# One-hot operands of an adjacency build: source split into tile and place, eight edge tiles at a time

## The chip, the cores and the metric

The kernel runs on one core of a Trainium2 chip. TensorE (PE in the profile, PEld for its weight loads), VectorE (DVE), ScalarE (ACT), GpSimd (POOL) and SyncE (SP) have instruction streams of their own and wait for each other by semaphores. The metric is the device time of one execution in microseconds, and the time of a kernel is the median over its runs.

## The reference

Two layers of a graph network with 1250 nodes, 768 features and 40,000 edges; each layer has a graph part, an attention part and a feed-forward part. The edges come sorted by destination. What the change touches is how the edges are used. In the first layer's graph part an edge counts as often as it occurs (and each node has a loop), in the second it counts with its weight:

```python
src, dst, edge_weight            # (40000,) each; dst is sorted
# layer 0, GAT: softmax over the edges that end in a node
e = leaky_relu(al_s[src] + al_d[dst], 0.2)
ex = exp(e - segment_max(e, dst)[dst])
out = segment_sum(h[src] * (ex / segment_sum(ex, dst)[dst])[:, :, None], dst)
# layer 1, GCN: weighted sums
deg = segment_sum(edge_weight, col) + 1.0
norm = rsqrt(deg)[row] * edge_weight * rsqrt(deg)[col]
agg = segment_sum(norm[:, None] * x[row], col)
```

The kernel turns the edges into two dense 1250 x 1250 matrices first, the number of edges from each source to each destination (CT) and the sum of their weights (WA, with ones on the diagonal), and works with those from there on.

## The kernel before

The edges lie as 313 tiles of 128 (`ET`), one edge per partition: `src_c`, `dst_c` and the weight as three bf16 parts `w_c[0..2]` that sum up to it, a column per edge tile. `NB` = 40 blocks of `SPREAD` = 8 tiles follow each other. As the edges are sorted, the destinations of a block lie in a window of `WIN` = 38 nodes, which begins at `base`; a test before the loop (`viol`, `flag`) sees whether that holds, and otherwise all engines take another loop, in which each block goes through all edges. Both loops call the same functions.

For one block, each engine in a loop over 20 pairs of blocks (`par` 0 and 1 are the two halves of the buffers):

- DVE, `destinations`: one operation (L1645) compares the destinations of the eight tiles with the window, which gives a one-hot of 8 x 38 columns, and three (L1651) multiply it with the three weight parts. So a tile has 4 x 38 = 152 columns (`KINDS` = 4). `next_block` (L1664) moves the window. `sources`, for seven of the eight tiles (L1660): the source of each edge against the numbers 0 to 1249, a one-hot of 1250 fp16 columns, into a ring of eight places.
- ACT, `source`: the one-hot of the eighth tile by two operations over 1250 columns (L1304, L1306).
- PE, `edge_tiles` (L890): for each tile and each of the ten groups of 125 source nodes, the one-hot of the group is the stationary operand and the 152 destination columns stream past it. That is 10 matmuls a tile and 80 a block, summed up in four banks of PSUM per half.
- ACT, `stage_block`: copies the block's sums from PSUM to `stage` (L1316, L1318), when PE is through and POOL has left the half.
- POOL, `unstage`: adds the three weight parts up (L749, L752) and adds count and weight into CT and WA at the window (L750, L756), four operations over 125 x 380.

What sets the order: PE waits tile by tile for its one-hot (`src_hot`, and `src_hot_act` for the eighth); DVE waits for `tiles_done`, so that a place in the ring is free; ACT waits for PE and POOL, POOL for ACT. Before the loop stands the setup: edges are loaded, turned by PE and copied (L1598 to L1637), with DVE waiting for its own last step by `chain`, while POOL fills constants and zeroes CT and WA (L731, L732). Behind the loop follows a layer norm: DVE's statistics of x (L1689) need nothing of the loop; its writing (L1701) goes to the memory in which the one-hots lie and waits for the last block's copy.

Of the kernel before, what the change touches and what calls it, by code (L numbers as in the profile page):

```python
# [46 lines left out]
RING = 8  # L47
# [168 lines left out]
def build(nc: bass.Bass, A, out):  # L216
    packets, pieces, last, packet_at = make_plan()

    with ExitStack() as ctx:
# [61 lines left out]
        def ecut(n):  # L281
# [21 lines left out]
        rawf = ecut(9 * P).rearrange("p (a r e) -> p a r e", a=3, r=3)  # L303
        ecut(2 * NT * KINDS * WIN - 18 * P)
        stage = xt_r[0:TILE, stage0:stage0 + 2 * NT * KINDS * WIN].rearrange("p (b j k w) -> p b j k w", b=2, j=NT, k=KINDS)
        oh_src = h_r[:, 0:RING * 625].bitcast(FP16).rearrange("p (s n) -> p s n", s=RING)
        oh_dst = h_r[:, 5000:5000 + SPREAD * KINDS * WIN].bitcast(BF16)\
            .rearrange("p (b t k w) -> p b t k w", b=2, t=SPREAD, k=KINDS)
# [391 lines left out]
        def _(pool):  # L700
# [27 lines left out]
            pool.sem_inc(ev("staged"), 4)  # L728
# [14 lines left out]
            def unstage(b, par, done):  # L743

                at = pool.value_load(basei[0:1, bass.ds(b, 1)], min_val=0, max_val=LAST)
                c = bass.ds(at, WIN)
                pool.wait_ge(ev("staged"), done * 2 + 6)
                k = stage[:, par]
                pool.tensor_tensor(k[:, :, 3, :], k[:, :, 3, :], k[:, :, 2, :], ALU.add).then_inc(ev("unst_b"), 1)  # L749
                pool.tensor_tensor(CT[:, :, c], CT[:, :, c], k[:, :, 0, :], ALU.add).then_inc(ev("unst_a"), 1)  # L750
                pool.wait_ge(ev("unst_b"), done + 1)
                pool.tensor_tensor(k[:, :, 3, :], k[:, :, 3, :], k[:, :, 1, :], ALU.add).then_inc(ev("unst_c"), 1)  # L752
                pool.wait_ge(ev("unst_a"), done + 1)
                pool.wait_ge(ev("unst_c"), done + 1)
                pool.wait_ge(ev("unstaged"), done + 2)
                pool.tensor_tensor(WA[:, :, c], WA[:, :, c], k[:, :, 3, :], ALU.add).then_inc(ev("unstaged"), 1)  # L756
# [87 lines left out]
        def _(pe):  # L844
# [32 lines left out]
            def bank(par, q):  # L877
                return ps[0:TILE, 2 * par + q // 2, 512 * (q % 2):512 * (q % 2) + 512]

            def edge_tiles(par, n, fresh):  # L880

                for u in range(SPREAD):
                    if u < SPREAD - 1:
                        pe.wait_ge(ev("src_hot"), n * (SPREAD - 1) + (u + 1))
                    else:
                        pe.wait_ge(ev("src_hot_act"), n + 1)
                    s = u % RING
                    for j in range(NT):
                        o = KINDS * WIN * (j % 3)
                        mm = pe.matmul(bank(par, j // 3)[:, o:o + KINDS * WIN], oh_src[:, s, j * TILE:j * TILE + TILE],  # L890
                                       oh_dst[:, par, u, :, :], start=(fresh and u == 0 and j % 3 == 0), stop=False,
                                       skip_group_check=True)
                    mm.then_inc(ev("tiles_done"), 1)

            def open_block(par, b):

                pe.wait_ge(ev("staged"), b * 2 + 2)

            def clear(par):
                for q in range(4):  # L900
                    w = KINDS * WIN * (3 if q < 3 else 1)
                    pe.matmul(bank(par, q)[:, 0:w], zero16[:, 0:TILE], zero16[:, 0:w], start=True, stop=False,
                              skip_group_check=True)

            with pe.If(flag == 0):
                with pe.Fori(0, NB // 2) as bp:
                    for par in range(2):
                        b = bp * 2 + par
                        open_block(par, b)
                        pe.wait_ge(ev("dst_hot"), b + 1)  # L910
                        edge_tiles(par, b, True)
            with pe.Else():
# [377 lines left out]
        def _(act):  # L1290
# [10 lines left out]
            def source(col, n):  # L1301

                act.wait_ge(ev("tiles_done"), n * SPREAD + CREDIT)
                act.activation(far, iota_src, ACT.Abs, bias=src_n[:, bass.ds(col, 1)]).then_inc(ev("src_far"), 1)  # L1304
                act.wait_ge(ev("src_far"), n + 1)
                act.activation(oh_src[:, RING - 1, :], far, ACT.Relu, bias=onesc, scale=-1.0)\  # L1306
                   .then_inc(ev("src_hot_act"), 1)

            def stage_block(par, b, tiles):
# [944 lines left out]
```

## Time and profile before

| | us |
|---|---|
| median of 3 runs | 3161.21 (3160.83 to 3163.68) |
| the profiled execution | 3162.54 |
| its span, first to last instruction | 3160.8 |
| setup, to DVE's first L1645 | 35.2 |
| adjacency loop, to the end of DVE's last L1660 | 306.7 |
| rest | 2818.9 |

All figures are of one core. In a row of windows the stretch comes first, then its length, then the busy time and the number of operations of PE, PEld, DVE, ACT and POOL, then the granted clock of TensorE as a share of full speed (1.00 is 2.4 GHz, 0.50 is 1.2 GHz), the busy share of the DMA engines and GB/s. In a timeline a row has start, length, engine, line, operation, output and inputs, shape and count; operations of one line that follow each other are one row, and the records of two neighbours overlap a little, so that the pace of an engine is read from start to start.

### The profile page before, as it was taken

What the parts mean: (1) busy time and instruction counts of PE and PEld (TensorE: products, weight loads), DVE (VectorE), ACT (ScalarE), POOL (GpSimd) and SP (SyncE); (2) the same over time, 40 slices, a digit from 0 to 9 for tenths busy, and PEclk for the clock granted to TensorE, in tenths of its full rate; (3) what the DMA queues carried; (4) which work ended last, traced back from release to release, by engine and by line L of the source; (5) the groups of instructions that cost most, each with busy time, mean ns of one, the idle gap of its engine ahead of it and who ended that gap; (6) DMA issues with size and microseconds to landing.
All of it is one profiled execution on the core that took longest, in us unless ns stands there. A gap on an engine that the chain in (4) does not pass through costs nothing.

```text
span 3160.8 us, 33593 instructions
## 1 busy us (share of the span) xinstructions
PE 2801.1 (89%) x13527; PEld 1971.8 (62%) x13527; DVE 1612.7 (51%) x2217; ACT 923.6 (29%) x974; POOL 333.0 (11%) x314
## 2 busy tenths in 40 slices
PE   4777899999989889699956989996879999899999
PEld 4777565688876556477743855553457777555555
DVE  8999679889973444311133230004267777522220
ACT  3666310077751232111110011011054444321110
POOL 5556230000000011100030000000000000000000
PEclk9999999999999899799976999997989999999999
DMA  9700431121030301477755100000020100200000
GB/s 248 265 0 0 110 94 59 42 71 57 34 64 6 84 7 52 140 250 261 259 150 115 33 17 0 30 30 29 0 80 27 40 27 29 105 10 10 10 10 10
DMA packets 123619, 226.60 MB, mean 72 GB/s; under 512 B 18535, under 2 KB 91788, under 8 KB 123006
## 3 DMA queue, kind: packets, MB, share of 16 engines
q1 hardware_dynamic: 107746, 178.79, 19.0%
q0 software_dynamic: 15760, 46.20, 4.6%
q8 instruction: 84, 1.38, 0.2%
q14 instruction: 29, 0.24, 0.0%
HBM read 158.92 MB, written 66.01 MB: 71 GB/s over the span
## 4 chain that ended last, share of the span: by engine, by line
PE 72%; DVE 18%; issue 3%; DMA 3%; ACT 2%; DVEq 1%; POOL 1%; SPq 0%; ACTq 0%; POOLq 0%
PE ps L939 20%; PE ps L1283 13%; PE ps L1267 13%; DVE arena L1660 5%; PE ps L1163 4%; PE ps L1129 4%; PE ps L956 4%; PE ps L1175 4%; DVE arena L1790 2%; DVE arena L1791 2%; PE ps L1216 1%; DVE small L1689 1%; PE ps L1208 1%; PE ps L1039 1%; DMA arena<-in_x_dram 1%
## 5 line engine op out<-in xcount | busy, mean ns | idle before, releaser
L939 PE MATMUL ps<-arena 128*125 128x384 f32 x2160 | 719.8, 496 | 28.3 <-DVE arena L2124 12.8
L939 PEld LDWEIGHTS ps<-arena 128*125 128x125 f32 x2160 | 412.4, 192 | 324.7 <-issue 34.5
L1283 PE MATMUL ps<-arena 128*125 128x384 f32 x1280 | 414.5, 488 | 14.2 <-DVE arena L2164 14.2
L1267 PE MATMUL ps<-arena 128*128 128x312 f32 (+1 forms) x1536 | 407.2, 428 | 15.2 <-DVE arena L2164 15.2
L1267 PEld LDWEIGHTS ps<-arena 128*128 128x128 f32 x1536 | 292.5, 191 | 129.6 <-issue 16.8
L1283 PEld LDWEIGHTS ps<-arena 128*125 128x125 f32 x1280 | 241.0, 188 | 187.6 <-issue 16.1
L1295 ACT ACTIVATE arena<-ps 128x750 f32<-128x750 f32 (+4 forms) x175 | 133.2, 792 | 722.0 <-PE ps L939 206.3
L890 PE MATMUL ps<-arena 128*125 128x152 bf16 x3200 | 244.2, 234 | 67.2 <-DVE arena L1660 65.6
L2164 DVE SCALAR_TENSOR_TENSOR arena<-arena 128x1250 f32<-128x1250 f32 (+1 forms) x170 | 231.4, 1383 | 114.5 <-PE ps L1267 110.9
L890 PEld LDWEIGHTS ps<-arena 128*125 128x125 f16 x3200 | 222.8, 138 | 88.6 <-DVE arena L1660 87.7
L1727 DVE SCALAR_TENSOR_TENSOR arena<-ps,arena 125x768 f32<-125x768 f32 x30 | 28.7, 956 | 379.1 <-PE ps L1283 291.9
L1660 DVE TENSOR_SCALAR arena<-arena 128x1250 f16<-128x1250 f16 x280 | 218.2, 850 | 0.0
L1039 PE MATMUL ps<-arena 125*125 125x97 f32 x1600 | 182.9, 276 | 5.7 <-DVE arena L1791 5.7
L1039 PEld LDWEIGHTS ps<-arena 125*125 125x125 f32 x1600 | 181.0, 192 | 9.0 <-DVE arena L1791 6.9
L2080 DVE TENSOR_TENSOR arena<-ps,arena 128x768 f32<-128x768 f32 x34 | 32.6, 958 | 271.3 <-PE ps L1175 271.3
L956 PE MATMUL ps<-arena 128*128 128x312 f32 (+7 forms) x544 | 156.6, 449 | 3.2 <-ACT arena L1295 2.2
L1129 PE MATMUL ps<-arena 125*125 125x385 f32 (+1 forms) x400 | 136.4, 497 | 11.3 <-POOL arena L821 11.3
L1783 DVE CUSTOM_DVE_ANT_0 arena<-arena 125x1250 bf16<-125x1250 bf16 x90 | 131.4, 1460 | 23.6 <-DMA arena<-al_src 21.0
L1163 PE MATMUL ps<-arena 128*128 128x256 f32 x612 | 136.8, 383 | 1.1 <-ACT arena L1295 1.1
L1175 PE MATMUL ps<-arena 128*128 128x384 f32 x408 | 134.5, 486 | 0.8 <-ACT arena L1295 0.8
L956 PEld LDWEIGHTS ps<-arena 128*128 128x128 f32 (+3 forms) x544 | 102.7, 191 | 52.1 <-issue 18.2
L1163 PEld LDWEIGHTS ps<-arena 128*128 128x128 f32 x612 | 117.7, 193 | 21.1 <-issue 1.5
(296 smaller groups left out, 2875.2 us busy)
## 6 DMA issues: line engine op xcount, KB each, us to landing
arena<-in_L_ffn_W_dram SPq DMA_DIRECT2D x34, 1152.0 KB, 7.0
xs_rows<-arena SPq DMA_DIRECT2D x1, 30720.0 KB, 99.5
arena<-xs_rows SPq DMA_DIRECT2D x17, 768.0 KB, 7.9
y_rows<-arena POOLq DMA_DIRECT2D x34, 384.0 KB, 3.3
arena<-in_kw_dram SPq DMA_DIRECT2D x24, 512.0 KB, 5.7
arena<-al_dst POOLq DMA_DIRECT2D x18, 625.0 KB, 4.9
arena<-in_kw_dram SPq DMA_DIRECT2D x6, 1536.0 KB, 9.9
arena<-in_x_dram SPq DMA_DIRECT2D x2, 3600.0 KB
```

Source lines behind the costliest of these rows:

```text
L890: mm = pe.matmul(bank(par, j // 3)[:, o:o + KINDS * WIN], oh_src[:, s, j * TILE:j * TILE + TILE], oh_dst[:, par, u, :, :], start=(fresh an ...
L939: mm = pe.matmul(slot(g)[0:TILE, 512 * half:512 * half + HALF], xt[:, k, i * TILE:i * TILE + TILE], w[:, k, :], start=(k == 0), stop=(k == ...
L956: mm = pe.matmul(slot(g)[0:rows, 512 * b:512 * b + w], stat, mov[:, lo + b * w:lo + b * w + w], start=(t == 0), stop=(t == len(terms) - 1))
L1039: mm = pe.matmul(slot(g)[0:TILE, 512 * (j // 5) + 97 * (j % 5):512 * (j // 5) + 97 * (j % 5) + 97], AT[m % AHEAD][:, j * TILE:j * TILE + T ...
L1129: mm = pe.matmul(slot(g)[0:TILE, 512 * b:512 * b + w], AT2[i][:, j * TILE:j * TILE + TILE], H769[:, i, lo:lo + w], start=(i == 0), stop=(i ...
L1163: mm = pe.matmul(slot(g)[:, 0:TAU], w1s[t % 2][:, k, f * P:f * P + P], xsT[t % 2][:, k, :], start=(k == 0), stop=(k == KT - 1))
L1175: mm = pe.matmul(slot(g)[:, 512 * b:512 * b + HALF], hTt[t % 2][:, f, h * P:h * P + P], w2s[t % 2][:, f, b * HALF:b * HALF + HALF], start= ...
L1267: mm = pe.matmul(slot(g)[:, 512 * b:512 * b + wd_], w[:, r % 2, ORDER[p], o * P:o * P + P], feat[place(f)][:, lo + b * wd_:lo + b * wd_ + ...
L1283: mm = pe.matmul(slot(g)[0:TILE, 512 * b:512 * b + HALF], fv[:, q, :], w2c[m][q][:, b * HALF:b * HALF + HALF], start=(p == 0 and q == 0), ...
L1295: give(act.activation(dst, src, func, **kw), g)
L1660: dve.tensor_scalar(oh_src[:, u % RING, :], iota_src, src_c[:, bass.ds(col + u, 1)], None, ALU.is_equal).then_inc(ev("src_hot"), 1)
L2164: return dve.scalar_tensor_tensor(out=out_, in0=in_, scalar=edge, in1=of, op0=op, op1=ALU.mult)
```

## The change

The one-hot of a source is split. A source s is in tile g = s // 125 and at place s - 125 g. The stationary operand is now the one-hot of the place alone (125 columns), once plain and three times multiplied with a part of the weight; the streamed operand is the one-hot of 38 g + (destination - window), 10 x 38 = 380 columns (`SPOTS`). A tile so has 4 matmuls of 380 columns instead of 10 of 152. The three weight parts are summed up in PSUM (the second bank of the half), so that a half holds two banks, one for the count and one for the weight, and POOL has two additions instead of four. The parts of the weight are kept as f32 (`w_p`), rounded through bf16.

DVE makes the four kinds of stationary operand for eight tiles at a time, by one comparison and three multiplications over 8 x 125 = 1000 elements, and then the eight streamed operands one by one. ACT makes no one-hots any more. The setup gets `group` (nine steps, each adding one where the source is at or over 125 t), `member` and `spot_of`. Both halves have a place of their own for all eight tiles, so that DVE waits for the tiles two blocks back.

```diff
@@ pool: constants, and into the matrices @@
-            own.step(pool.iota(iota_src, [[1, NODES]], base=0, channel_multiplier=0,
+            own.step(pool.iota(spots, [[1, SPOTS]], base=0, channel_multiplier=0,
                                allow_small_or_imprecise_dtypes=True))
-            own.step(pool.iota(iota_0, [[1, WIN]], base=0, channel_multiplier=0,
+            own.step(pool.iota(within, [[1, TILE]], base=0, channel_multiplier=0,
                                allow_small_or_imprecise_dtypes=True))
...
-                pool.wait_ge(ev("staged"), done * 2 + 6)
+                pool.wait_ge(ev("staged"), done + 3)
                 k = stage[:, par]
-                pool.tensor_tensor(k[:, :, 3, :], k[:, :, 3, :], k[:, :, 2, :], ALU.add).then_inc(ev("unst_b"), 1)
-                pool.tensor_tensor(CT[:, :, c], CT[:, :, c], k[:, :, 0, :], ALU.add).then_inc(ev("unst_a"), 1)
-                pool.wait_ge(ev("unst_b"), done + 1)
-                pool.tensor_tensor(k[:, :, 3, :], k[:, :, 3, :], k[:, :, 1, :], ALU.add).then_inc(ev("unst_c"), 1)
+                pool.tensor_tensor(CT[:, :, c], CT[:, :, c], k[:, 0], ALU.add).then_inc(ev("unst_a"), 1)
                 pool.wait_ge(ev("unst_a"), done + 1)
-                pool.wait_ge(ev("unst_c"), done + 1)
                 pool.wait_ge(ev("unstaged"), done + 2)
-                pool.tensor_tensor(WA[:, :, c], WA[:, :, c], k[:, :, 3, :], ALU.add).then_inc(ev("unstaged"), 1)
+                pool.tensor_tensor(WA[:, :, c], WA[:, :, c], k[:, 1], ALU.add).then_inc(ev("unstaged"), 1)
@@ tensor @@
                 for u in range(SPREAD):
...
-                    for j in range(NT):
-                        o = KINDS * WIN * (j % 3)
-                        mm = pe.matmul(bank(par, j // 3)[:, o:o + KINDS * WIN], oh_src[:, s, j * TILE:j * TILE + TILE],
-                                       oh_dst[:, par, u, :, :], start=(fresh and u == 0 and j % 3 == 0), stop=False,
-                                       skip_group_check=True)
+                    pe.wait_ge(ev("hot"), n * SPREAD + (u + 1))
+                    for k in range(KINDS):
+                        mm = pe.matmul(bank(par, min(k, 1)), oh_src[:, par, u, k, :], oh_spot[:, par, u, :],
+                                       start=(fresh and u == 0 and k < 2), stop=False, skip_group_check=True)
                     mm.then_inc(ev("tiles_done"), 1)
@@ scalar: source() is gone, one copy of 2 x 380 from PSUM @@
-                act.activation(dst[:, 0:9 * w].rearrange("p (b n) -> p b n", b=3), src[:, 0:3, 0:3 * w], ACT.Copy)\
+                act.activation(stage[:, par].rearrange("p k j w -> p k (j w)"), banks_of(par), ACT.Copy)\
                    .then_inc(ev("staged"), 1)
-                act.activation(dst[:, 9 * w:10 * w], src[:, 3, 0:w], ACT.Copy).then_inc(ev("staged"), 1)
@@ vector: setup @@
-            own.step(dve.tensor_scalar(src_n, ps[:, 0, 0:NB * SPREAD], -1.0, None, ALU.mult))
+            own.step(dve.memset(group, 0.0))
             own.settle()
 
-            chain(dve.tensor_copy(w_c[0], w_f))
-            chain(dve.tensor_tensor(w_f, w_f, w_c[0], ALU.subtract))
-            chain(dve.tensor_copy(w_c[1], w_f))
-            chain(dve.tensor_tensor(w_f, w_f, w_c[1], ALU.subtract))
-            chain(dve.tensor_copy(w_c[2], w_f))
+            for k in range(3):
+                chain(dve.tensor_copy(w_16, w_f))
+                chain(dve.tensor_copy(w_p[k], w_16))
+                if k < 2:
+                    chain(dve.tensor_tensor(w_f, w_f, w_p[k], ALU.subtract))
+            for t in range(1, NT):
+                chain(dve.scalar_tensor_tensor(out=group, in0=src_c, scalar=float(t * TILE), in1=group,
+                                               op0=ALU.is_ge, op1=ALU.add))
+            chain(dve.scalar_tensor_tensor(out=member, in0=group, scalar=-float(TILE), in1=src_c,
+                                           op0=ALU.mult, op1=ALU.add))
...
-            dve.tensor_scalar(iota_b, iota_0, base[:, 0:1], None, ALU.add).then_inc(ev("next_block"), 1)
+            chain(dve.scalar_tensor_tensor(out=grouped(spot_of), in0=grouped(group), scalar=float(WIN), in1=grouped(offset),
+                                           op0=ALU.mult, op1=ALU.add))
@@ vector: the block; destinations(), sources() and next_block() are gone @@
+            def one_hots(par, col, tile0, ring, spot, n):
+
+                dve.wait_ge(ev("tiles_done"), tile0 + (SPREAD - ring + CREDIT))
+                wide = [P, SPREAD, TILE]
+                dve.tensor_tensor(oh_src[:, par, :, 0, :], within.unsqueeze(1).broadcast_to(wide),
+                                  member[:, bass.ds(col, SPREAD)].unsqueeze(2).broadcast_to(wide), ALU.is_equal)\
+                   .then_inc(ev("plain"), 1)
+                dve.wait_ge(ev("plain"), n + 1)
                 for k in range(3):
+                    dve.tensor_tensor(oh_src[:, par, :, 1 + k, :], oh_src[:, par, :, 0, :],
+                                      w_p[k][:, bass.ds(col, SPREAD)].unsqueeze(2).broadcast_to(wide), ALU.mult)
+                for u in range(SPREAD):
+                    dve.tensor_scalar(oh_spot[:, par, u, :], spots, spot(u), None, ALU.is_equal).then_inc(ev("hot"), 1)
```

`keys`, which makes the same numbers for the other loop (unsorted edges), isn't shown.

How the instructions stand, first on DVE in the first block of the loop. ISA and REGISTER_ALU are steps of the engine's own sequencer; `ev_tiles_done` counts tiles that PE is through with. Before, to the second L1660:

```order
L1645 ISA [waits ev_tiles_done]
L1645 TENSOR_TENSOR arena<-arena 128x8x38
L1651 ISA [waits ev_dst_plain]
L1651 TENSOR_TENSOR arena<-arena 128x8x38
L1651 ISA
L1651 TENSOR_TENSOR arena<-arena 128x8x38
L1651 ISA
L1651 TENSOR_TENSOR arena<-arena 128x8x38
L1664 ISA
L1664 TENSOR_SCALAR arena<-arena 128x38
L1659 REGISTER_ALU
L1660 ISA [waits ev_tiles_done]
```

Behind it stand seven of the 128x1250 operations, each with such a wait. After, to the second of eight L1637:

```order
L1629 ISA [waits ev_tiles_done]
L1629 TENSOR_TENSOR arena<-arena 128x8x125
L1632 REGISTER_ALU
L1634 ISA [waits ev_plain]
L1634 TENSOR_TENSOR arena<-arena 128x8x125
L1634 ISA
L1634 TENSOR_TENSOR arena<-arena 128x8x125
L1634 ISA
L1634 TENSOR_TENSOR arena<-arena 128x8x125
L1637 ISA
L1637 TENSOR_SCALAR arena<-arena 128x380
L1637 ISA
```

The operations with two tensor inputs grow from 304 to 1000 elements; the one-source operations behind them are eight over 380 instead of seven over 1250, and only the block's first step waits for PE.

On POOL, one block of the loop. Before:

```order
L749 TENSOR_TENSOR arena<-arena 125x10x38 [waits ev_staged]
L750 ISA
L750 TENSOR_TENSOR arena<-arena 125x10x38
L751 REGISTER_ALU
L752 TENSOR_TENSOR arena<-arena 125x10x38 [waits ev_unst_b]
L755 REGISTER_ALU [waits ev_unst_c,ev_unst_a]
L756 ISA [waits ev_unstaged]
L756 TENSOR_TENSOR arena<-arena 125x10x38
```

After:

```order
L753 ISA [waits ev_staged]
L753 TENSOR_TENSOR arena<-arena 125x10x38
L754 REGISTER_ALU
L755 REGISTER_ALU [waits ev_unst_a]
L756 ISA [waits ev_unstaged]
L756 TENSOR_TENSOR arena<-arena 125x10x38
```

The two additions within `stage` are gone, the two into the matrices remain.

## Rows read from the trace of the kernel before

**Rows 1.** The page, busy tenths of DVE in 40 slices of 79 us.

```profile
DVE  8999679889973444311133230004267777522220
```

**Rows 2.** Windows: the adjacency loop; columns as told above.

```profile
35.19:341.90 306.71, 242.41 (x3176) 221.13 (x3177) 300.85 (x481) 188.47 (x178) 180.27 (x156) 0.99 0.35 118
```

**Rows 3.** Waits from 37 to 342 us: total, times, longest.

```profile
ACT arena L1316 <- PE ps L890: 114.5, 39, 6.6
...
PE ps L890 <- DVE arena L1660: 65.6, 97, 5.5
```

**Rows 4.** Timeline of DVE, the first two blocks of the loop.

```profile
35.19 0.48 DVE L1645 TENSOR_TENSOR arena<-arena 128x304 bf16<-128x304 f32 x1 [1.45 <-issue]
35.81 1.25 DVE L1651 TENSOR_TENSOR arena<-arena 128x304 bf16<-128x304 bf16 x3
36.97 0.24 DVE L1664 TENSOR_SCALAR arena<-arena 128x38 f32<-128x38 f32 x1
37.12 3.27 DVE L1660 TENSOR_SCALAR arena<-arena 128x1250 f16<-128x1250 f16 x7
40.31 0.47 DVE L1645 TENSOR_TENSOR arena<-arena 128x304 bf16<-128x304 f32 x1
...
45.64 0.48 DVE L1645 TENSOR_TENSOR arena<-arena 128x304 bf16<-128x304 f32 x1
```

**Rows 5.** Single lines: count, ns min/median/max, first and last start.

```profile
L1645 DVE TENSOR_TENSOR arena<-arena x40: 459/461/1267, 35.2 to 334.3; 128x304 bf16<-128x304 f32 x40
...
L1660 DVE TENSOR_SCALAR arena<-arena x280: 529/544/1285, 37.1 to 341.4; 128x1250 f16<-128x1250 f16 x140
```

**Rows 6.** Timeline from 54 to 57 us, DVE and POOL.

```profile
54.47 1.24 POOL L752 TENSOR_TENSOR arena<-arena 125x380 f32<-125x380 f32 x1
54.77 1.27 DVE L1645 TENSOR_TENSOR arena<-arena 128x304 bf16<-128x304 f32 x1
...
56.18 1.06 DVE L1651 TENSOR_TENSOR arena<-arena 128x304 bf16<-128x304 bf16 x1
```

**Rows 7.** Timeline of PE, the first blocks of the loop.

```profile
37.72 16.94 PE L890 MATMUL ps<-arena 128*125 128x152 bf16 x220 [5.47 <-DVE arena L1660]
```

**Rows 8.** Timeline of DVE in the setup.

```profile
27.01 0.56 DVE L1609 TENSOR_TENSOR arena<-arena 128x384 f32<-128x384 f32 x1
27.61 0.36 DVE L1610 CAST arena<-arena 128x384 bf16<-128x384 f32 x1
...
29.76 0.33 DVE L1623 TENSOR_SCALAR arena<-arena 128x320 f32<-128x320 f32 x1
...
32.48 0.20 DVE L1630 TENSOR_TENSOR arena<-arena 128x40 f32<-128x40 f32 x1
32.71 0.26 DVE L1631 SCALAR_TENSOR_TENSOR arena<-arena,small 128x40 f32<-128x40 f32 x1
33.02 0.18 DVE L1634 TENSOR_SCALAR arena<-arena 128x40 f32<-128x40 f32 x1
```

**Rows 9.** Groups by line, 344 to 350 us: busy us, mean ns, idle before.

```profile
L1689 DVE BATCH_NORM_STATS2 small<-arena 125x6 f32<-125x384 f32 x14 | 6.5, 539 | 0.0
...
L756 POOL TENSOR_TENSOR arena<-arena 125x380 f32 x1 | 1.0, 994 | 0.3 <-POOL arena L752 0.3
L750 POOL TENSOR_TENSOR arena<-arena 125x380 f32 x1 | 0.9, 873 | 0.0
```

**Rows 10.** Timeline of POOL in the setup.

```profile
2.96 1.18 POOL L711 IOTA arena<- 128x1250 f16 x1
...
10.74 10.98 POOL L732 MEMSET arena<- 125x12800 f32 x1
```

**Rows 11.** Windows around the fall of TensorE's clock in the loop.

```profile
52.60:59.39 6.79, 4.51 (x62) 4.05 (x61) 6.65 (x11) 5.78 (x6) 4.61 (x5) 1.00 1.05 363
59.39:62.80 3.41, 3.41 (x31) 3.41 (x30) 3.41 (x4) 1.85 (x2) 3.08 (x4) 0.50 1.04 360
62.80:335.00 272.20, 214.53 (x2834) 194.18 (x2833) 267.05 (x424) 167.22 (x158) 163.24 (x141) 1.00 0.29 98
```

More of the change, by code:

```diff
@@ L46 @@
 KINDS = 4
-RING = 8
+SPOTS = NT * WIN
 CREDIT = 32
@@ L284, in ecut @@
             return xt_r[:, eo[0] - n:eo[0]]
-        iota_src = ecut(625).bitcast(FP16)
+        spots = ecut(SPOTS // 2).bitcast(FP16)
+        within = ecut(64).bitcast(FP16)[:, 0:TILE]
         src_c = ecut(ECOLS)
         dst_c = ecut(ECOLS)
-        w_c = [ecut(ECOLS // 2).bitcast(BF16) for _ in range(3)]
+        w_p = [ecut(ECOLS) for _ in range(3)]
         w_f = ecut(ECOLS)
-        src_n = ecut(SPREAD * NB)
-        far = ecut(NODES // 2).bitcast(FP16)
+        w_16 = ecut(ECOLS // 2).bitcast(BF16)
+        group = ecut(ECOLS)
+        member = ecut(ECOLS)
+        offset = ecut(ECOLS)
         viol = ecut(ECOLS)
-        iota_0 = ecut(WIN)
-        iota_b = ecut(WIN)
+        spot_of = ecut(ECOLS)
+        spot8 = ecut(2 * SPREAD).rearrange("p (b t) -> p b t", b=2)
+        out8 = ecut(SPREAD)
+        off8 = ecut(SPREAD)
         zero16 = ecut(256).bitcast(BF16)
@@ L302, in build @@
         raw = ecut(9 * P).rearrange("p (a r e) -> p a r e", a=3, r=3)
[L303 to L308, printed above, removed]
+        stage = xt_r[0:TILE, stage0:stage0 + 4 * SPOTS].rearrange("p (b k j w) -> p b k j w", b=2, k=2, j=NT)
+        ecut(max(0, 4 * SPOTS - 9 * P))
+        rawf = h_r[:, 7040 - 9 * P:7040].rearrange("p (a r e) -> p a r e", a=3, r=3)
+        oh_src = h_r[:, 0:4000].bitcast(BF16).rearrange("p (b t k n) -> p b t k n", b=2, t=SPREAD, k=KINDS)
+        oh_spot = h_r[:, 4000:7040].bitcast(BF16).rearrange("p (b t n) -> p b t n", b=2, t=SPREAD)
         CT = ct_r[0:TILE, 0:6400].bitcast(FP16).rearrange("p (t n) -> p t n", t=NT)
@@ L1299, in _ @@
             flag = act.value_load(flagi[0:1, 0:1], min_val=0, max_val=EDGES)
[L1301 to L1307, printed above, removed]
             def stage_block(par, b, tiles):
@@ L1322, in _ @@
                     for par in range(2):
-                        source((bp * 2 + par) * SPREAD + (SPREAD - 1), bp * 2 + par)
                         stage_block(par, bp * 2 + par, SPREAD)
@@ L1327, in _ @@
                     for par in range(2):
-                        with act.Fori(0, CHUNKS) as ch:
-                            source(ch * SPREAD + (SPREAD - 1), (bp * 2 + par) * CHUNKS + ch)
                         stage_block(par, bp * 2 + par, SPREAD * CHUNKS)
@@ new lines, in keys @@
+            def keys(par, col, b, n):
+                own8 = ev("keys")
+                dve.tensor_scalar(off8, dst_c[:, bass.ds(col, SPREAD)], base[:, bass.ds(b, 1)], None, ALU.subtract)\
+                   .then_inc(own8, 1)
+                dve.wait_ge(own8, n * 5 + 1)
+                dve.tensor_scalar(out8, off8, 0.0, None, ALU.is_lt).then_inc(own8, 1)
+                dve.wait_ge(own8, n * 5 + 2)
+                dve.scalar_tensor_tensor(out=out8, in0=off8, scalar=float(WIN), in1=out8, op0=ALU.is_ge, op1=ALU.add)\
+                   .then_inc(own8, 1)
+                dve.scalar_tensor_tensor(out=off8, in0=group[:, bass.ds(col, SPREAD)], scalar=float(WIN), in1=off8,
+                                         op0=ALU.mult, op1=ALU.add).then_inc(own8, 1)
+                dve.wait_ge(own8, n * 5 + 4)
+                dve.scalar_tensor_tensor(out=spot8[:, par, :], in0=out8, scalar=-4096.0, in1=off8, op0=ALU.mult, op1=ALU.add)\
+                   .then_inc(own8, 1)
+                dve.wait_ge(own8, n * 5 + 5)
@@ L1669, in _ @@
                         b = bp * 2 + par
[L1670 to L1672 removed]
+                        one_hots(par, b * SPREAD, b * SPREAD, 2 * SPREAD, lambda u: spot_of[:, bass.ds(b * SPREAD + u, 1)], b)
             with dve.Else():
@@ L1678, in _ @@
                             n = b * CHUNKS + ch
-                            destinations(par, ch * SPREAD, n, n * SPREAD + CREDIT, b)
-                            sources(ch * SPREAD, n * SPREAD)
-                        next_block(b)
+                            keys(par, ch * SPREAD, b, n)
+                            one_hots(par, ch * SPREAD, n * SPREAD, SPREAD, lambda u: spot8[:, par, u:u + 1], n)
             norms = [0]
```

58 lines of the change are left out of this document (13 added, 45 removed).

## The prediction

> **What bounds the kernel now.** I read the page's slices first: VectorE (DVE) is busy 8 to 9 tenths of the first four slices [rows 1]. The stage in which the change lies, the adjacency loop, runs from 35.19 to 341.89 us, 306.7 us for 40 blocks of eight edge tiles; in it DVE is busy 300.9 us, PE 242.4, POOL 180.3, ACT 188.5 [rows 2]. Second, the waits of that stretch: PE waits 65.6 us for L1660, ACT 114.5 for PE [rows 3], and the view has no row in which DVE waits for anyone. So the loop goes at DVE's pace, and what counts is the sum of DVE's steps in a block, with whatever stretches them.
>
> Third, what stretches them. Before POOL has work, a block takes DVE 5.12 us and one with the loop's branch 5.33 (starts of L1645 at 35.19, 40.31, 45.64) [rows 4], 5.23 in the mean. Later, (334.3 - 45.64)/37 = 7.80 us [rows 5]. The operations are the same. The reader is to see the difference in two places: L1660 takes 529 ns at least and 1285 at most, L1645 459 and 1267 [rows 5]; and at 54.77 us an L1645 lasts until 56.04, 0.33 us beyond the end (55.71) of the POOL operation L752 that was there first, and the L1651 behind it takes 1.06 us, where three of them undisturbed take 1.25 [rows 4]. A DVE operation with POOL at work before it waits until POOL is done, one with two sources as well. The four POOL operations of a block cost (7.80 - 5.23)/4 = 0.64 us of DVE time each.
>
> **PE.** A block has the same columns before (80 x 152) and after (32 x 380), 12,160. Before, 220 matmuls in a row took 16.94 us [rows 7], 6.16 us a block. Longer ones have fewer starts, so 6.16 is the upper bound; at 2.4 GHz and a column a cycle 5.07 would be the lower. Both lie under DVE's old block and its new one: hidden behind DVE. ACT drops its two 1250-element operations and copies 760 elements in place of 1368 and 152: its waits are for PE [rows 3], so it is off the path before, and after all the more.
>
> **DVE in the new block, with POOL away.** Two-source operations: 384 elements take 0.560 us, 40 take 0.200 [rows 8], 1.047 ns an element, and the old 304 with bf16 and with f32 inputs take 0.47 to 0.48 alike [rows 4]; the new ones read a broadcast f32 operand as well. From 304 to 1000 elements is 0.73 us more.
> - The comparison L1629: old step with the wait behind it 0.62 us (35.19 to 35.81), new 1.35.
> - Three multiplications L1634: old step (36.97 - 35.81)/3 = 0.387, new 1.12 each, 3.35.
> - Eight spot one-hots L1637 of 380 fp16 elements, one source. The 1250-element steps are (40.31 - 37.12)/7 = 0.456 us, the 38-element step 0.15 [rows 4]: 0.252 ns an element, so 0.15 + 342 x 0.252 = 0.236 us each, 1.89. That is the lower bound; f32 one-source operations (320 elements 0.33, 40 elements 0.18 [rows 8]) have 0.53 ns an element, 0.33 us each; at the two-source rate it would be 0.51. I take 0.236: input and output are 2 bytes wide as in L1660, only that the output is bf16.
> - The next-block step (L1664, 0.15) goes.
>
> Sum 6.59, with the branch's (5.33 - 5.12)/2 = 0.10 it is 6.69 us, against 5.23. By its own work DVE thus loses 1.46 us a block: seven operations at four elements in a nanosecond give way to 4000 elements at one.
>
> **What POOL gives back.** Two of four POOL operations go (L749, L752); left are the additions into the matrices, L750 (now L753) and L756, 0.87 and 0.99 us undisturbed [rows 9]. They have the shape of the two that go, so I take the old 0.64 us each, 1.29 a block. Bounds: a start-to-start of 56.18 - 54.77 = 1.41 where 0.62 was undisturbed, 0.79 each [rows 4, 6]; below, 0.34, if half of the hold falls into times in which DVE waits anyway (the 0.3 us behind the comparison). Steady block: 6.69 + 1.29 = 7.98 us. Saved are two collisions, 1.29 us; lost 1.46. The first two blocks run without POOL, as before: 2 x 6.69 + 38 x 7.98 = 316.6 us, **+9.9**.
>
> A DVE operation reading one source outside the fast modes isn't stretched: L1689 keeps 539 ns while POOL works [rows 9]. The Trainium skill (SBUF — State Buffer, Who interferes with whom) has the rule: a VectorE operation with two SBUF inputs contends with a GpSimd operation that reads SBUF, whoever starts first keeps the port for its whole length, and an operation with one input outside the two-port modes doesn't. Rows 6 and 9 agree. By the page's "whole length" the two would cost 0.87 and 0.99 us, the block 8.55, the sum 3200; the rows have less, since DVE's own gaps take a part.
>
> **Setup.** DVE's chain from 24.7 to 35.2 us stands ahead of the loop with nearly every step waiting for the one before [rows 8]. Added: ten three-operand operations over 384 elements, at a step of 0.60 (27.01 to 27.61) and perhaps 0.06 more (L1631 0.26 against L1630 0.20): 6.3; one over 320, 0.5; three casts like L1610, 0.36 and the gap of 0.04, 1.2. Removed: L1636, a step like that of L1664, 0.15; L1605 and the memset in its place I take as even. Together +7.9. POOL's iota over 1250 elements (1.18 us) and one over 38 become 380 and 125: 0.94 ns for each of 783 fewer elements, up to 0.7 us, and DVE's second cast waits for the end of POOL's memset at 21.72 (10.74 + 10.98) [rows 10], so -0.7. **+7.2**.
>
> **Behind the loop** nothing is gained: DVE's statistics (L1689, fourteen in 6.5 us [rows 9] and twenty in all, then the mean and root) are some 10 us of work of its own before it writes where the one-hots lie; PE's last block, at most 6.2 us, and the copy of ACT fit under that.
>
> Sum: +9.9 + 7.2 = +17.1 on the profiled execution's 3162.5 (span 3160.8 and 1.7 around it): 3179.6. That execution lies 1.3 us above the median, so **3178 us**. DVE waits for PE only two blocks back (16 tiles), which 6.2 us of PE work in 7.98 never reaches.
>
> **Rivals.**
> 1. *POOL collides less.* It works about 2 us a block, and its operations could fall into the wait behind the comparison or the gaps of the one-hots. The sum is -31.9 us + 76 x the cost of one. At 0.34 each the block is 7.37 and the time 3155, at 0.15 each 7.0 and 3141. The result is within 0.2% between steady blocks of 7.37 and 7.69 (0.34 to 0.50 each), and break-even is 7.53, 0.42 each. For it: in a block of mostly long operations POOL waits at a boundary more often, and one of four boundaries is the wait of 0.3. Against it: the old loop paid 0.64 with gaps of the same number, and L1645 and L1651 were delayed in full [rows 6]. Faster, below 7.37: 0.10; within: 0.14.
> 2. *The spot one-hots miss the fast rate* (bf16 out of fp16). At 0.33 each +0.75 a block, 3208; at 0.51 each +2.2, 3266. No row has this pair of types. 0.07.
> 3. *PE's clock falls and PE becomes the bound.* With PE busy 4.51 of 6.79 us (66%) the clock fell to half (1.2 GHz) from 59.39 to 62.80 us, with 79% it stayed at full for 272 us [rows 11]. The new loop has 64 to 77%. At half clock the columns need 10.13 us a block: 40 x 10.13 = 405, 3267. Against it: that low stretch ended by itself, PE being busy in all of it [rows 11]; PE needs only 5.07/7.98 = 64% of full clock on average. [...] 0.04.
> 4. *The change doesn't do what it says*, the loop taken being the one for unsorted edges, 40 times as many tiles: far over 10,000 us. The test on the edges is unchanged. Under 0.01.
>
> **How the numbers follow.** The forecast, 3168 to 3200 by collision costs of 0.50 to 0.93, has 0.65; the rivals 0.24, 0.07 and 0.04. A measurement here can tell 0.2%, 6.3 us, from no change. Slower by more: 0.65 + 0.11 = 0.76; same 0.14; faster 0.10. Range 3152 to 3204: below it 0.08, above it some 0.11.
>
> **What would show it.** Step by step in the profile after: L1629 about 1.2 us undisturbed and up to 2.0 beside POOL; L1634 1.17; L1637 about 0.3 us long and 0.24 from start to start (0.33 or 0.51 is rival 2); starts of L1629 7.98 apart; DVE's first L1629 at 42.3 us; PE waiting for L1637 about 2 us a block and DVE for nobody. A block under 7.4 us would make me wrong on POOL; PE's clock under 0.65 in the stage with DVE waiting for PE is rival 3.

## The result

| | us |
|---|---|
| before, median of 9 runs | 3161.92 (3156.88 to 3163.68) |
| after, median of 9 runs | 3170.94 (3165.07 to 3174.91) |
| ratio, 95% interval | 1.0028 (1.0018 to 1.0039) |
| the profiled execution of after, its span | 3169.12, 3167.4 |

The changed kernel is slower by 9 us, 0.28%. The forecast was 3178 with a range of 3152 to 3204, slower by more than 0.2%; the direction and the range hold, the size was nearly twice as large (+17 against +9).

The page's slices of DVE, the granted clock below it, in the place of [rows 1]:

```profile
DVE  8999779979983454411124140003267777522220
...
PEclk9998899999999899799976999998989999899999
```

DVE is as full as before in the first four slices, and the clock, at 9 in all of the first five slices before, shows 8 in the fourth and the fifth. The loop and the rest as windows (length, busy us and operations of PE, PEld, DVE, ACT, POOL, then the clock), in the place of [rows 2]:

```profile
41.94:351.46 309.52, 239.02 (x1258) 185.19 (x1259) 303.82 (x481) 56.76 (x59) 110.48 (x77) 0.91 0.32 111
351.46:3167.40 2815.94, 2554.82 (x10338) 1749.33 (x10336) 1294.39 (x1710) 734.40 (x795) 127.39 (x126) 0.94 0.22 66
```

The loop takes 309.5 us instead of 306.7: DVE is busy in nearly all of it, while the busy time of ACT fell from 188.5 to 56.8 and that of POOL from 180.3 to 110.5. The setup ends at 41.94 instead of 35.19. The two are +2.8 and +6.75, +9.6 together, against +9.0 by the medians; the rest differs by 3 us in this pair of executions (2818.9 and 2815.9), which is inside the spread of the runs.

The waits from 40 to 350 us, in the place of [rows 3]:

```profile
ACT arena L1295 <- PE ps L885: 251.5, 39, 11.1
...
PE ps L885 <- DVE arena L1637: 73.7, 38, 8.3
```

The view still has no row in which DVE waits for another engine. The first blocks on DVE, with POOL not yet at work, in the place of [rows 4]:

```profile
41.94 1.21 DVE L1629 TENSOR_TENSOR arena<-arena 128x1000 bf16<-128x1000 f16 x1 [1.35 <-issue]
43.29 3.42 DVE L1634 TENSOR_TENSOR arena<-arena 128x1000 bf16<-128x1000 bf16 x3
46.63 1.92 DVE L1637 TENSOR_SCALAR arena<-arena 128x380 bf16<-128x380 f16 x8
48.46 1.20 DVE L1629 TENSOR_TENSOR arena<-arena 128x1000 bf16<-128x1000 f16 x1
...
54.97 1.19 DVE L1629 TENSOR_TENSOR arena<-arena 128x1000 bf16<-128x1000 f16 x1
```

A block is 6.52 and 6.51 us, and its parts are 1.35, 3.34 (1.113 each) and 1.83 (0.229 each). Later blocks take (344.9 - 54.97)/37 = 7.84 us in the mean; most of them are close to one of 6.5, 7.9 and 9.0 us, by how many POOL operations fall into them. Single lines (ns min/median/max, first and last start), in the place of [rows 5]:

```profile
L1629 DVE TENSOR_TENSOR arena<-arena x40: 1186/1192/1205, 41.9 to 344.9; 128x1000 bf16<-128x1000 f16 x40
L1634 DVE TENSOR_TENSOR arena<-arena x120: 1184/1196/1926, 43.3 to 348.4; 128x1000 bf16<-128x1000 bf16 x120
L1637 DVE TENSOR_SCALAR arena<-arena x320: 302/310/1042, 46.6 to 351.1; 128x380 bf16<-128x380 f16 x160
L753 POOL TENSOR_TENSOR arena<-arena x40: 868/1742/2584, 55.1 to 356.3; 125x380 f32 x40
```

Now POOL waits more for DVE (L753 needs 868 ns and takes up to 2584), and DVE for POOL as before, but in L1634 and L1637 alone. Counted one by one in the trace, 23 of the 120 L1634 and 53 of the 320 L1637 are stretched, 76 in all, as many as POOL has additions in the loop (two in each of 38 blocks). How one collision looks, in the timeline of after from 150 us:

```profile
151.14 3.42 DVE L1634 TENSOR_TENSOR arena<-arena 128x1000 bf16<-128x1000 bf16 x3
...
153.37 1.91 POOL L753 TENSOR_TENSOR arena<-arena 125x380 f32 x1 [3.83 <-ACT arena L1295]
154.47 3.26 DVE L1637 TENSOR_SCALAR arena<-arena 128x380 bf16<-128x380 f16 x8
...
155.54 0.93 POOL L756 TENSOR_TENSOR arena<-arena 125x380 f32 x1 [0.26 <-POOL arena L753]
157.65 1.19 DVE L1629 TENSOR_TENSOR arena<-arena 128x1000 bf16<-128x1000 f16 x1
```

L753 begins at 153.37, when the third multiplication has just begun, and its 0.87 us of work end only at 155.28; the first L1637 behind that multiplication is the one that is stretched (to 0.93 us), and another one is beside L756 (to 1.04). The eight one-hots take 3.26 us instead of 1.92.

### The profile page after: what moved, and what is told of

It reads as the page before. It is cut to its first block, busy times and chain, and to the rows that moved or that the text cites. A ratio compares the mean times of both kernels' runs of the same rounds, so it can differ in the third digit from the quotient of the medians.

```text
span 3167.4 us, 29186 instructions
## 1 busy us (share of the span) xinstructions
PE 2797.2 (88%) x11607; PEld 1937.3 (61%) x11607; DVE 1627.3 (51%) x2230; ACT 791.4 (25%) x854; POOL 260.5 (8%) x234
## 3 DMA queue, kind: packets, MB, share of 16 engines
q8 instruction: 83, 1.36, 0.2%
## 4 chain that ended last, share of the span: by engine, by line
PE 73%; DVE 17%; issue 3%; DMA 3%; ACT 2%; DVEq 1%; POOL 1%; SPq 0%; ACTq 0%; POOLq 0%
PE ps L929 20%; PE ps L1273 13%; PE ps L1257 13%; PE ps L1153 4%; PE ps L1119 4%; PE ps L1165 4%; PE ps L946 4%; DVE arena L1637 3%; DVE arena L1777 2%; PE ps L885 2%; DVE arena L1778 2%; DVE arena L1634 2%; PE ps L1206 1%; PE ps L1029 1%; DVE small L1676 1%
## 5 line engine op out<-in xcount | busy, mean ns | idle before, releaser
L929 PE MATMUL ps<-arena 128*125 128x384 f32 x2160 | 714.5, 493 | 30.9 <-issue 14.6
L1273 PEld LDWEIGHTS ps<-arena 128*125 128x125 f32 x1280 | 241.6, 189 | 188.5 <-issue 17.4
L885 PE MATMUL ps<-arena 128*125 128x380 bf16 x1280 | 242.8, 354 | 73.7 <-DVE arena L1637 73.7
L2151 DVE SCALAR_TENSOR_TENSOR arena<-arena 128x1250 f32<-128x1250 f32 (+1 forms) x170 | 231.4, 1383 | 114.0 <-PE ps L1257 110.5
L885 PEld LDWEIGHTS ps<-arena 128*125 128x125 bf16 x1280 | 188.1, 150 | 128.2 <-DVE arena L1637 86.6
L1634 DVE TENSOR_TENSOR arena<-arena 128x1000 bf16<-128x1000 bf16 x120 | 150.3, 1307 | 5.7
```

The source lines that it names most:

```text
L885: mm = pe.matmul(bank(par, min(k, 1)), oh_src[:, par, u, k, :], oh_spot[:, par, u, :], start=(fresh and u == 0 and k < 2), stop=False, ski ...
L929: mm = pe.matmul(slot(g)[0:TILE, 512 * half:512 * half + HALF], xt[:, k, i * TILE:i * TILE + TILE], w[:, k, :], start=(k == 0), stop=(k == ...
L1273: mm = pe.matmul(slot(g)[0:TILE, 512 * b:512 * b + HALF], fv[:, q, :], w2c[m][q][:, b * HALF:b * HALF + HALF], start=(p == 0 and q == 0), ...
L1634: dve.tensor_tensor(oh_src[:, par, :, 1 + k, :], oh_src[:, par, :, 0, :], w_p[k][:, bass.ds(col, SPREAD)].unsqueeze(2).broadcast_to(wide), ...
L2151: return dve.scalar_tensor_tensor(out=out_, in0=in_, scalar=edge, in1=of, op0=op, op1=ALU.mult)
```

## The experiments

The theory: DVE bounds the loop, and a block takes DVE's own work plus a fixed price for each POOL operation with tensor inputs. The rivals: other traffic stretches the blocks; the collisions saturate; TensorE's clock costs something; part of the setup is hidden. Each ratio is to runs of the kernel before in the same series, whose median was 3159.7 us for e1 to e4, 3160.4 for e5 to e8 and 3159.1 for e9 and e10.

**e1, POOL's additions over one element, in the changed kernel.**

```diff
-    pool.memset(ct_r[0:TILE, 0:6400], 0.0)
+    pool.memset(ct_r[0:TILE, 0:6400], 0.007826805114746094)
...
-    pool.tensor_tensor(CT[:, :, c], CT[:, :, c], k[:, 0], ALU.add)
+    pool.tensor_tensor(CT[:, 0:1, bass.ds(at, 1)], CT[:, 0:1, bass.ds(at, 1)], k[:, 0, 0:1, 0:1], ALU.add)
-    pool.tensor_tensor(WA[:, :, c], WA[:, :, c], k[:, 1], ALU.add)
+    pool.tensor_tensor(WA[:, 0:1, bass.ds(at, 1)], WA[:, 0:1, bass.ds(at, 1)], k[:, 1, 0:1, 0:1], ALU.add)
```

(The new constant is the f32 number that fills memory with fp16 ones.)

> The changed kernel, with POOL's two additions of a block over one element instead of 125 x 380; the matrices are left at constants, so the graph parts don't compute the reference. Theory (DVE bounds the loop, a block is its own work of 6.52 us plus 0.66 us for each collision with POOL): starts of L1629 6.5 to 6.7 us apart, the loop 261 to 268 us instead of 309.5, the time 3122 to 3130 us. Rival (the blocks of 7.9 and 9.0 us come from something else: memory traffic of PE, ACT or DMA, or DVE's code): blocks stay at 7.8 in the mean, the time at 3171.

Measured: 3120.6 us, ratio to before 0.9875 (0.9858 to 0.9891), 50 us under the changed kernel and 1.4 under the range expected. Its loop, and L1629 and L1637 in it:

```profile
41.94:302.37 260.43, 212.47 (x1258) 169.52 (x1259) 254.73 (x481) 56.73 (x59) 22.69 (x78) 1.00 0.38 131
...
L1629 DVE TENSOR_TENSOR arena<-arena x40: 1191/1195/1204, 41.9 to 295.8; 128x1000 bf16<-128x1000 f16 x40
...
L1637 DVE TENSOR_SCALAR arena<-arena x320: 307/311/318, 46.6 to 302.1; 128x380 bf16<-128x380 f16 x160
```

(295.8 - 41.9)/39 = 6.51 us a block, as in the first two blocks of the changed kernel, and no L1637 longer than 318 ns. All of the 49.1 us between 309.5 and 260.4 are POOL's doing, in 76 operations (38 blocks of two): 0.65 us each. The work of PE and ACT and the transfers are the same, so the first rival falls.

**e2, two more POOL additions a block.**

```diff
                 k = stage[:, par]
+                for q in range(2):
+                    pool.tensor_tensor(waste, k[:, 0], k[:, 1], ALU.add).then_inc(ev("unst_b"), 1)
+                    pool.wait_ge(ev("unst_b"), done * 2 + (q + 1))
```

> The changed kernel, with two more POOL additions over 125 x 380 in each block, ahead of the two that are there, into a scratch tile. Theory (each POOL operation costs DVE 0.66 us): a block of 6.52 + 4 x 0.66 = 9.16 us, the loop 13 + 38 x 9.16 = 361 us, the time 3171 + 52 = 3223 us. Rival (collisions saturate, since POOL fits in the gaps between DVE's long operations): half of that or less, at most 3197 us.

Measured: 3230.4 us, ratio 1.0222 (1.0205 to 1.0239).

```profile
41.95:408.05 366.10, 263.57 (x1258) 201.29 (x1259) 360.29 (x481) 56.72 (x59) 194.56 (x153) 0.83 0.27 94
```

The loop is 366.1 us, 56.6 more for 76 operations, 0.74 us each; against e1 all four cost 105.7/152 = 0.70. So the price doesn't saturate. The time is 7 us over the 3223 expected, and the profiled execution (3223.9) lies 6.5 us under the median, so that by the medians the two additional operations cost 0.78 us each.

**e3, POOL's four additions over one element, in the kernel before.** The edit is that of e1 for L749, L750, L752 and L756.

> The kernel before, with POOL's four additions of a block over one element; the matrices are left at constants. Theory: DVE's own work is 5.23 us a block, below PE's 6.16, so PE becomes the bound at 6.2 to 6.4 us a block, the loop 248 to 258 us instead of 306.7, the time 3103 to 3113 us. Rival (POOL isn't what stretches): 3162.

Measured: 3084.7 us, ratio 0.9760 (0.9744 to 0.9776), 75 us under the kernel before and 18 us under the range expected. From the waits, the loop, and DVE's first blocks:

```profile
DVE arena L1645 <- PE ps L890: 23.0, 18, 1.3
...
PE ps L890 <- ACT arena L1306: 19.0, 19, 1.0
...
35.20:267.26 232.06, 210.78 (x3110) 207.82 (x3110) 202.17 (x481) 184.24 (x174) 62.10 (x152) 1.00 0.46 156
...
35.20 0.47 DVE L1645 TENSOR_TENSOR arena<-arena 128x304 bf16<-128x304 f32 x1 [1.45 <-issue]
...
40.32 0.47 DVE L1645 TENSOR_TENSOR arena<-arena 128x304 bf16<-128x304 f32 x1
...
45.43 0.47 DVE L1645 TENSOR_TENSOR arena<-arena 128x304 bf16<-128x304 f32 x1
```

Without POOL the old loop takes 232 us, 5.8 a block, and DVE isn't alone as the bound any more: PE waits for ACT's one-hot, DVE for PE. I had expected PE at 6.2; it is busy 210.8/40 = 5.27 us a block (3110 of its 3200 matmuls are in the trace). The first two blocks take 5.12 and 5.11 us, DVE's own work before, without the 0.2 us that [rows 4] show on the second. So the own work went from 5.11 to 6.51 us, +1.40, and a collision cost (7.80 - 5.11)/4 = 0.67 us before and (7.84 - 6.51)/2 = 0.66 after.

**e4, the setup's additions alone, in the kernel before** (the last one, over 320 elements as for `spot_of`, is left out below).

```diff
             chain(dve.tensor_copy(w_c[2], w_f))
+            for k in range(3):
+                chain(dve.tensor_copy(w_f, w_c[k]))
+            chain(dve.memset(w_f, 0.0))
+            for t in range(1, NT):
+                chain(dve.scalar_tensor_tensor(out=w_f, in0=src_c, scalar=float(t * TILE), in1=w_f,
+                                               op0=ALU.is_ge, op1=ALU.add))
+            chain(dve.scalar_tensor_tensor(out=w_f, in0=w_f, scalar=-float(TILE), in1=src_c,
+                                           op0=ALU.mult, op1=ALU.add))
...
```

> The kernel before, with the changed kernel's extra setup on DVE (three casts, a memset, ten three-operand operations over 384 elements and one over 320, each waiting for the one before) into a scratch tile whose content isn't used. Theory (the setup is on the path): 3 x 0.39 + 0.41 + 10 x 0.59 + 0.53 = +8.0 us, 3170 us, DVE's first L1645 8.0 us later than 35.19. Rival (part of it is hidden): less than +4.

Measured: 3168.1 us, ratio 1.0025 (1.0015 to 1.0036), +8.5 us. The rows of the added part and the loop's first:

```profile
29.00 1.16 DVE L1614 CAST arena<-arena 128x384 f32<-128x384 bf16 x3
30.30 0.38 DVE L1615 MEMSET arena<- 128x384 f32 x1
30.71 5.32 DVE L1617 SCALAR_TENSOR_TENSOR arena<-arena 128x384 f32<-128x384 f32 x9
...
43.38 0.48 DVE L1655 TENSOR_TENSOR arena<-arena 128x304 bf16<-128x304 f32 x1 [1.45 <-issue]
```

The loop starts 8.2 us later, and all of that is in the time. The changed kernel's setup costs 6.75 of it, since L1605 and L1636 go and POOL's shorter rows of numbers bring the end of DVE's second cast, and all behind it, forward by 0.66 us. So of the change's +9 us some seven are setup, two or three the loop.

This run also tells what the 0.2 us of [rows 4] are. Its third block starts 5.61 us behind the second, and the profile names PE as what DVE waited for. First the third block here, then the same moment in the kernel before:

```profile
53.89 1.31 ACT L1316 ACTIVATE arena<-ps 125x1368 f32<-125x1368 f32 x1 [6.84 <-PE ps L890]
54.11 0.48 DVE L1655 TENSOR_TENSOR arena<-arena 128x304 bf16<-128x304 f32 x1 [0.21 <-PE ps L890]
```

```profile
45.43 1.31 ACT L1316 ACTIVATE arena<-ps 125x1368 f32<-125x1368 f32 x1 [6.57 <-PE ps L890]
45.64 0.48 DVE L1645 TENSOR_TENSOR arena<-arena 128x304 bf16<-128x304 f32 x1
```

ACT's copy and DVE's third block wait for the same thing, PE's eight tiles of the first block, and in both kernels DVE starts 0.21 to 0.22 us behind ACT. PE was late with them because its matmuls went at half pace at first: in the kernel before 33 of them took 4.14 us (37.72 to 41.86), and later 49 took 3.08 (42.32 to 45.40). In e3 the fast pace came 0.46 us sooner (ten matmuls from 41.86 to 42.32 instead of six), ACT's copy began at 45.21 and DVE's third block at 45.43, where its own pace has it too: the 0.2 us aren't there. So [rows 4] show no branch of the loop but a wait for PE, once, at the start of the loop.

**e5, the compared row in f32.**

```diff
-        spots = ecut(SPOTS // 2).bitcast(FP16)
+        spots = ecut(SPOTS)
```

> The changed kernel, with the row of numbers that L1637 compares held as f32 instead of fp16 (the output stays bf16). Theory (the one-source operations run at four elements in a nanosecond only with 2-byte input and output, and DVE's sum is the loop): a step of 0.33 us instead of 0.229, eight of them +0.8 us a block, the loop 309.5 + 32 = 341 us, the time 3203 us. Rival (DVE has slack, or the rate doesn't depend on the input's width): 3171 us.

Measured: 3200.1 us, ratio 1.0120 (1.0105 to 1.0136), 3 us under the 3203 expected.

```profile
L1637 DVE TENSOR_SCALAR arena<-arena x320: 403/411/1082, 46.6 to 381.9; 128x380 bf16<-128x380 f32 x160
```

The operation is 0.1 us longer (403 against 302 ns at least), 320 times, and the loop takes 340.4 us, +30.9. This is what the second rival of the prediction would have cost, and it shows that DVE has no slack in the loop.

**e6, PE filled with matmuls of zeros.**

```diff
+                for _ in range(8 if fresh else 0):
+                    pe.matmul(bank(par, 0), zero16[:, 0:TILE], zero16[:, 0:SPOTS], start=True, stop=False,
+                              skip_group_check=True)
                 for u in range(SPREAD):
```

> The changed kernel, with eight more matmuls of zeros over 380 columns (1.3 us) in front of each block's matmuls, where PE has nothing to do. Theory (the falls of TensorE's clock in the loop, 15 of them, cost nothing, as DVE never waits for PE): the granted clock stays near 1.00 in the loop, the blocks at 7.8 us, the time at 3168 to 3174 us. Rival (the clock's falls cost something): faster than 3165.

Measured: 3172.5 us, ratio 1.0037 (1.0023 to 1.0051). First windows of the changed kernel, then the loop of e6:

```profile
67.45:70.86 3.41, 1.26 (x8) 1.09 (x9) 3.41 (x6) 0.56 (x1) 2.16 (x2) 1.00 1.01 354
70.86:74.28 3.42, 3.42 (x13) 2.44 (x12) 3.28 (x8) 0.00 (x0) 0.00 (x0) 0.50 1.00 350
74.28:84.52 10.24, 7.73 (x47) 5.99 (x45) 10.10 (x16) 2.89 (x3) 4.26 (x3) 1.00 1.00 348
84.52:87.93 3.41, 2.85 (x9) 2.12 (x10) 3.41 (x9) 0.00 (x0) 1.31 (x2) 0.50 1.00 348
```

```profile
41.95:354.52 312.57, 266.67 (x1582) 214.46 (x1583) 306.87 (x481) 56.76 (x59) 88.33 (x78) 1.00 0.31 110
```

In the changed kernel the clock falls to 1.2 GHz 16 times in the loop (once before). It fell at 70.86 after a stretch in which PE had little to do (1.26 us of 3.41), and it rose after stretches in which PE was busy throughout (3.42 of 3.42) or for the most part (2.85 of 3.41): 0.91 in the mean of the loop. With the filling it stays at 1.00, and nothing is gained: 3172.5 against 3170.9 us, both within the spread of either kernel. The third rival named a thing that does happen, and that costs nothing here, where PE catches up within DVE's block.

**e7, two fp16 parts of the weight and a short setup.** As DVE's own work is the price of the change, the next question is what can be taken off it. `w_p` has two parts, and `w_16`, `oh_src` and `oh_spot` are fp16.

```diff
-KINDS = 4
+KINDS = 3
...
-            for t in range(1, NT):
-                chain(dve.scalar_tensor_tensor(out=group, in0=src_c, scalar=float(t * TILE), in1=group,
-                                               op0=ALU.is_ge, op1=ALU.add))
+            chain(dve.tensor_scalar(group, src_c, float(TILE // 2), 1.0 / TILE, ALU.subtract, ALU.mult))
+            chain(dve.tensor_scalar(group, group, 12582912.0, 12582912.0, ALU.add, ALU.subtract))
```

> The changed kernel, with the weight in two fp16 parts instead of three bf16 parts (one multiplication on DVE and one matmul of four less), and the source's tile by one scaling and one rounding step in the setup instead of nine comparisons. Theory: DVE's own work 6.51 - 1.11 = 5.40 us a block, with the same 1.32 for POOL 6.72, the loop 10.8 + 38 x 6.72 = 266 us, setup 6.3 us shorter, the time 3171 - 43 - 6 = 3122 us. Rival (with shorter blocks PE or ACT becomes the bound, or POOL collides more often): 3135 or above.

Measured: 3121.0 us, ratio 0.9872 (0.9856 to 0.9887), as expected to 1 us. DVE's first block:

```profile
35.59 1.20 DVE L1627 TENSOR_TENSOR arena<-arena 128x1000 f16<-128x1000 f16 x1 [1.35 <-issue]
36.94 2.31 DVE L1632 TENSOR_TENSOR arena<-arena 128x1000 f16<-128x1000 f16 x2
39.16 1.92 DVE L1635 TENSOR_SCALAR arena<-arena 128x380 f16<-128x380 f16 x8
40.99 1.20 DVE L1627 TENSOR_TENSOR arena<-arena 128x1000 f16<-128x1000 f16 x1
```

The setup is 6.35 us shorter than in the changed kernel (35.59 against 41.94) and a block of DVE's own work 1.11 (5.40 against 6.51).

**e8, ACT makes two of the eight streamed one-hots.** In the changed loop ACT waits 251.5 us for PE. This run and the next two build on e7. `NACT` is 2, and `spot_n` is `spot_of` negated.

```diff
+            def spots_act(par, b):
+                act.wait_ge(ev("tiles_done"), b * SPREAD + (CREDIT - SPREAD))
+                for q in range(NACT):
+                    u = SPREAD - NACT + q
+                    act.activation(far, spots, ACT.Abs, bias=spot_n[:, bass.ds(b * SPREAD + u, 1)])\
+                       .then_inc(ev("spot_far"), 1)
...
+                    act.activation(oh_spot[:, par, u, :], far, ACT.Relu, bias=onesc, scale=-1.0)\
+                       .then_inc(ev("hot_act"), 1)
```

> The kernel with two fp16 parts and the short setup, and the streamed one-hots of two of the eight tiles made by ACT by two operations over 380 columns each. Theory: two steps of 0.229 us less on DVE, 6.26 us a block, ACT at some 4 us a block under it; 40 x 0.46 = 18 us less, the time 3104 us. Rival (PE waits for ACT's one-hots, as ACT copies the block before first): no gain over 3122 or a loss.

Measured: 3103.9 us, ratio 0.9819 (0.9806 to 0.9832), 17 us under e7 and as expected. The loop:

```profile
35.96:285.00 249.04, 180.97 (x946) 131.87 (x947) 243.33 (x361) 152.39 (x219) 92.75 (x78) 0.95 0.42 145
```

**e9 and e10, three and four of the eight on ACT.** `NACT` is 3 and 4.

> As with two streamed one-hots on ACT, but three of the eight. Theory: DVE's own work 4.70 us, with POOL 6.03 us a block instead of 6.29; ACT needs three times 1.39 us, 0.9 for the copy and half a table load of 1.28, 5.7 us, still under DVE: 10 us less, 3094 us. Rival (ACT is already close enough that its one-hots come late and PE and DVE wait): 3104 or above.

> As before, but four of the eight on ACT. Theory: ACT becomes the bound: 4 x 1.39 + 0.9 + 0.64 = 7.1 us a block against DVE's 5.8, the loop 284 us, 3139 us, and DVE waiting for PE. Rival (DVE stays the bound, ACT's work overlaps better than its sum): 3085 us.

Measured: 3102.8 us (0.9822, 0.9809 to 0.9835) and 3161.4 us (1.0002, 0.9993 to 1.0012). From the waits from 60 to 240 us, e9 first, then e10:

```profile
PE ps L892 <- ACT arena L1306: 44.9, 63, 1.0
...
DVE arena L1648 <- PE ps L892: 11.3, 15, 1.1
```

```profile
PE ps L892 <- ACT arena L1306: 53.7, 73, 1.5
DVE arena L1648 <- PE ps L892: 48.8, 23, 3.1
```

With three, PE already waits for ACT and DVE for PE, and the third gains nothing: 3102.8 us is where the rival of e9 had it (3104), not its theory (3094). With four all that e7 and e8 had gained is gone, and neither expectation holds: the theory had 3139 us. The loop takes 305.8 us, 7.6 a block, where ACT's sum gives 7.1. ACT's one-hots for a block start only when the copy of the block before is through, which waits for PE, which waits for ACT; that this ring adds the rest follows from the code and the two waits, it wasn't tried apart. The version of e8 is faster than both kernels, by 56 us than the one before (3160.4 in the same series) and by 67 than the changed one.

## Why the prediction was right, and where it was off

- **DVE bounds the loop; PE and ACT are hidden.** Right. No wait of DVE in the changed loop, e5 adds its full price, e6 with more PE work and a full clock changes nothing. The upper bound for PE, 6.16 us, was loose (5.27 in e3): it was read from 220 matmuls of which the first went at half pace (e4). It carried nothing here, but made the expectation of e3 too high by 18 us and more.
- **DVE's own work, 6.69 us a block.** Here the sum was off: 6.51. The comparison (1.35) and the multiplications (3.34 against 3.35) came to the hundredth; the one-hots were 1.83 instead of 1.89. The term that was wrong is the loop's branch: I read the 5.33 us between the second and third L1645 of [rows 4] as a branch of 0.21 in every second block, and neither e3 (5.12, 5.11) nor the new loop (6.52, 6.51) has it. They were a wait for PE, once (e4). The 0.18 us too much in 40 blocks are 7 of the 8 us by which the forecast was too high, 4 of them the branch and some 2.4 the one-hots. The same interval stands in the 5.23 us of the old block, and so made a collision a little too cheap there (0.64 us for 0.67).
- **POOL, 0.64 us an operation.** Right: 0.65 by e1, 0.66 by the blocks. The first rival, collisions that fall into DVE's waits, didn't come about. The two multipliers of the sum, -31.9 + 76 x the cost, would have been -39 + 76 x the cost with the right own work: at 0.65, +10; the loop and setup measured +9.6.
- **The signs in the profile.** The first L1629 (41.94 for 42.3), the one-hots' step (0.229 for 0.24) and PE's waits (73.7/38 = 1.9 us a block for 2) came as said, the blocks shorter (7.84 for 7.98). L1629 was to last up to 2.0 us beside POOL and never did (1205 ns at most).
- **Setup, +7.2.** Measured +6.75 and in the time in full (e4).
- **The clock.** It fell as the row of [rows 11] hinted, 16 times in the loop, and the reason given why it wouldn't count held (e6).
- **The sum.** The loop's +9.9 was +2.8; the whole +17.1 was +9.0. In the loop two large terms nearly cancel: 1.40 us more of DVE's own work a block, and 2.69 - 1.33 = 1.36 us less for POOL. That the loop came out slower at all hangs on 0.07 us a block, less than the sum could tell, and the forecast had the larger part of the loss there, while it was the smaller one. That the direction came out right is due to the setup for the most part.

## What to carry to other kernels

Halving an engine's work helps nothing where another engine's sum bounds the loop: ACT lost 132 us of busy time here and nothing came of it. POOL lost 70, and what that gave back was only what its two additions had taken from DVE, 1.36 us a block. DVE's own sum grew by 1.40: its one-source work, at four elements in a nanosecond, fell from 8750 elements a block to 3040, and its two-source work, at one, rose from 1216 to 4000. Where VectorE and GpSimd work side by side, price a GpSimd operation with tensor inputs twice, once on its own engine and once as time of VectorE (some two thirds of a microsecond for the 125 x 380 additions here; other sizes weren't tried, except for one element, which cost nothing that shows). And read a repeated overhead from more than one pair of rows, and ask what else ends at that moment: a single odd interval, taken for a branch, was the largest error of this forecast, and it was a wait that occurs once.

## What was not expected of the hardware

- The price of a collision hardly depends on what DVE does: 0.67 us in blocks of 304- and 1250-element operations, 0.66 in blocks of 1000- and 380-element ones, 0.70 with four POOL operations beside the long ones. It is 0.2 to 0.3 under POOL's undisturbed length of 0.87 and 0.99 us. What grows beside DVE's longer operations is POOL's own time: L753 takes up to 2.58 us, while none of the old kernel's four took more than 1.33.
- L1629, one of the four long operations, was never delayed in the changed kernel (1186 to 1205 ns in 40; with four POOL additions, in e2, two of 40 were), though it reads two tensors as L1634 does, which was, and though in 12 of the 40 an operation of POOL was under way beside it. Nine times L753 had begun 0.6 us before L1629 and went on until 1.9 us after L1629's start, and the L1634 behind it was the one that was stretched:

```profile
108.87 2.55 POOL L753 TENSOR_TENSOR arena<-arena 125x380 f32 x1 [7.05 <-ACT arena L1295]
109.50 1.19 DVE L1629 TENSOR_TENSOR arena<-arena 128x1000 bf16<-128x1000 f16 x1
110.84 3.48 DVE L1634 TENSOR_TENSOR arena<-arena 128x1000 bf16<-128x1000 bf16 x2
```

So here it wasn't the operation that began first that went first, as the prediction had it. Why is open.
- A comparison with 2-byte input and output keeps the fast rate across types (fp16 in, bf16 out, 380 elements in a step of 0.229 us), while an f32 input adds 0.1 us.
